# A new order for the attention period of a fused macaron block: two small operations change engine, one turn in the first feed-forward half comes a slot later

## The reference, cut to what matters

```
x = x + 0.5 * ffn(layernorm(x))          # shared SwiGLU + routed SwiGLU, 8 experts, top 1
x = x + attention(layernorm(x))          # (8, 512, 256), 16 heads of 16, 64 landmarks
x = x + 0.5 * ffn(layernorm(x))

# attention, for each of 8 batches
q_l, k_l = means of q, k over 8 neighbouring tokens          # landmarks
s1 = softmax(q @ k_l.T); s2 = softmax(q_l @ k_l.T); s3 = softmax(q_l @ k.T)
z = s2.T / (col * row)                                        # largest row and column sums
for _ in range(6):
    xz = s2 @ z
    z = 0.25 * z @ (13 I - xz @ (15 I - xz @ (7 I - xz)))
out = (s1 @ (z @ (s3 @ v))) @ Wo + bo
```

## Time and profile before

| | |
|---|---|
| median of 3 runs | 1190.49 us (1188.29 to 1193.56) |
| the profiled execution's own time | 1187.06 us |
| its span, first to last instruction | 1185.3 us |
| PE busy | 1096.0 us, 92% |
| DVE busy | 767.7 us, 65% |
| ACT busy | 581.3 us, 49% |
| POOL busy | 557.4 us, 47% |
| mean granted clock of PE | 0.970 of full speed |

### The profile page before, as it was taken

How to read it: one execution, slowest core, us unless ns; L and a number is a source line. 1 busy time by engine, 2 the same in 40 slices (tenths; PEclk the granted TensorE clock), 3 DMA queues, 4 the chain that set the end, 5 groups by cost and what they waited for, 6 DMA issues and landing times.

```text
span 1185.3 us, 30048 instructions
## 1 busy us (share of the span) xinstructions
PE 1096.0 (92%) x11278; PEld 886.9 (75%) x11279; DVE 767.7 (65%) x1425; ACT 581.3 (49%) x937; POOL 557.4 (47%) x774
## 2 busy tenths in 40 slices
PE   8999999999998778889889898879999999999997
PEld 6788887888887556667667676658888888888886
DVE  5746557767675755867877967545446566776764
ACT  4334246666664445355355453334434246666663
POOL 5710815666665623344434522224600717666664
PEclk8999999999999788999999998779999999999999
DMA  7181143222210400000000000012440142122220
GB/s 248 72 328 63 36 181 110 69 71 65 63 57 25 131 14 2 3 3 2 3 2 3 2 3 2 2 38 107 161 178 19 60 176 67 58 67 62 70 64 18
DMA packets 39472, 80.25 MB, mean 68 GB/s; under 512 B 6452, under 2 KB 31159, under 8 KB 38336
## 3 DMA queue, kind: packets, MB, share of 16 engines
q1 hardware_dynamic: 27568, 52.94, 12.4%
q0 software_dynamic: 11232, 25.20, 6.9%
q10 hardware_dynamic: 560, 0.52, 0.1%
HBM read 57.13 MB, written 27.00 MB: 71 GB/s over the span
## 4 chain that ended last, share of the span: by engine, by line
PE 78%; DVE 12%; ACT 3%; issue 3%; POOL 3%; DMA 1%; ACTq 0%; POOLq 0%; DVEq 0%; SPq 0%
PE PS L1730 18%; PE PS L1644 14%; PE PS L1744 12%; PE PS L1660 7%; PE PS L1737 3%; PE PS L1818 3%; DVE A_NM L805 3%; PE PS L1928 2%; PE PS L1575 2%; DVE A_NM L798 2%; PE PS L1678 2%; PE PS L1828 2%; PE PS L1941 2%; PE PS L1862 1%; PE PS L1671 1%
## 5 line engine op out<-in xcount | busy, mean ns | idle before, releaser
L1730 PE MATMUL PS<-WHL,XGH 128*128 128x512 f32 x624 | 217.6, 430 | 2.1 <-DVE WHL L676 2.1
L1485 POOL TENSOR_TENSOR A_W<-A_XC,CB 128x256 f32<-128x256 f32 x96 | 68.1, 730 | 207.3 <-DVE A_XC L891 181.3
L1744 PE MATMUL PS<-WD,XNT 128*128 x624 | 149.7, 383 | 1.5 <-ACT XNT L1135 1.5
L697 DVE SCALAR_TENSOR_TENSOR XNT<-PS,SCORES,XNT 128x512 f32<-128x512 f32 x78 | 58.6, 751 | 120.4 <-PE PS L1730 120.4
L1393 POOL DMA_INDIRECT X<-xs_dram,WHO x78 | 101.2, 1297 | 70.5 <-PE PS L1678 28.2
L1730 PEld LDWEIGHTS PS<-WHL,XGH 128*128 128x128 f32 x624 | 111.4, 189 | 20.2 <-DVE WHL L676 2.6
L1130 ACT ACTIVATE XNT<-PS,SCORES 128x512 f32<-128x512 f32 x78 | 53.7, 689 | 145.9 <-PE PS L1730 145.7
L1744 PEld LDWEIGHTS PS<-WD,XNT 128*128 128x128 f32 x624 | 112.6, 190 | 15.8 <-issue 2.0
L1730 PE MATMUL PS<-WHL,XGL 128*128 128x512 f32 x312 | 123.2, 395 | 0.0
L1387 POOL TENSOR_SCALAR XNT<-WD 128x128 f32<-128x128 f32 x64 | 49.2, 787 | 119.2 <-DVE WD L570 119.2
L1660 PE MATMUL PS<-SDH,HHL 128*128 128x256 f32 x512 | 103.7, 286 | 0.5 <-DVE X L610 0.5
(11 more groups left out here) (273 smaller groups left out, 2551.9 us busy)
## 6 DMA issues: line engine op xcount, KB each, us to landing
xs_dram<-WG SPq DMA_DIRECT2D x16, 512.0 KB, 3.0
WU<-in_r_up SPq DMA_DIRECT2D x2, 4096.0 KB, 14.8
shared_dram<-X SPq DMA_DIRECT2D x16, 512.0 KB, 3.3
WG<-in_r_gate SPq DMA_DIRECT2D x2, 4096.0 KB, 19.1
WD<-in_r_down SPq DMA_DIRECT2D x4, 2048.0 KB, 7.6
X<-in_x SPq DMA_DIRECT2D x7, 512.0 KB, 9.0
X<-mid_dram SPq DMA_DIRECT2D x7, 512.0 KB, 3.8
X<-xs_dram,WHO POOLq DMA_INDIRECT x78, 2.9
```

What stands on the lines that cost most here:

```text
L697: dve.scalar_tensor_tensor(B["RH"][:, u * F:(u + 1) * F], banks[3 + u][:], score(t), B["RS"][:, u * F:(u + 1) * F], ALU.mult, ALU.mult).th ...
L1485: pool.tensor_tensor(B["W"][:].rearrange("p (a m) -> p a m", m=M)[:, part, :], B["XC"][b % 2][:].rearrange("p (a w) -> p a w", w=XW)[:, pa ...
L1730: ins = pe.matmul(banks[bank][:], tok, w[:, k * F:(k + 1) * F], start=(k == 0 and i == 0), stop=(k == KD - 1 and i == 2))
L1744: ins = pe.matmul(banks[7][:, 0:D], B["HT"][:, u * F + f * P:u * F + (f + 1) * P], B["WD"][:, bass.ds(ex * (KF * D) + f * D, D)], start=(f ...
```

## The change

Nothing is computed differently. Five things change:

- PE's fillers stand in another order around the twelve products of a period, and so do DVE's and ACT's.
- `key_block` leaves DVE and becomes `key_landmarks` on ACT; `product_kept` (two copies of 128x64 out of PSUM) moves from DVE to ACT too.
- `column_max` is cut in three: the column maximum and its scaling stay, `pair_scale` (a reciprocal) comes between the two last reductions, and `masked_scale` (A_MR) moves into the next period, behind `chain_s(b, 3)`.
- The banks of turns and values are the same in all periods (turn k and value half jj in bank 6 + k, 6 + jj). Both halves of the values are projected behind the second round's second product; one half used to stand a round later.
- `TURN_SLOT` of groups 3 to 7 and everything behind them (logits, routing, table) comes one slot later, in both feed-forward halves. On POOL, `root(1, 0)` and `rows(1, 1)` of feed-forward 1 move behind other steps.

The core of the diff:

```diff
-    TURN_SLOT = {1: 2, 2: 4, 3: 5, 4: 7, 5: 8, 6: 9, 7: 10}
+    TURN_SLOT = {1: 2, 2: 4, 3: 6, 4: 8, 5: 9, 6: 10, 7: 11}
...
+            def key_landmarks(b):
+                act.wait_ge(att["lm"], count("lm", b, 4))
+                act.mul(B["KLS"][:], B["KL"][:], 1.0 / LM).then_inc(att["kls"], 1)
+
+            def product_kept(b):
+                act.wait_ge(att["tp_ready"], count("tp_ready", b, 1))
+                for c in range(KD):
+                    act.copy(B["XC"][b % 2][:].rearrange("p (a w) -> p a w", w=XW)[:, c * PC:(c + 1) * PC, M:],
+                             banks[c][:, 0:PC * HS].rearrange("p (a d) -> p a d", d=HS)).then_inc(att["tp"], 1)
...
                 chain_b(b, 2)
-                if exists(nxt) and nxt > 0:
-                    act.wait_ge(att["nm3_ready"], count("nm3_ready", nxt, 1))
-                    act.copy(B["NM3T"][:], banks[nm3_bank(nxt)][:, 0:P]).then_inc(att["nm3"], 1)
+                if exists(nxt):
+                    exp3(nxt, 0)
                 if exists(far):
                     projected(far, 0)
                     rounded(far, 0)
-                if exists(nxt):
-                    exp3(nxt, 0)
-                    if nxt > 0:
-                        values(nxt, 1)
...
                 chain_s(b, 4)
+                if exists(nxt):
+                    row_kept(nxt)
                 if exists(old):
                     heads_norm(old)
-                if exists(nxt):
-                    row_kept(nxt)
+                chain_x(b, 4)
+                if exists(nxt):
                     s1_max(nxt, 0, (0, 1))
-                chain_x(b, 4)
-                if exists(nxt):
-                    column_max(nxt)
-                    s1_max(nxt, 1, (0,))
                 chain_s(b, 5)
```

More of the change, by code:

```diff
@@ L855, in start_y @@
             def start_y(b):
+                dve.wait_ge(att["own"], count("own", b, 4))
                 dve.wait_ge(att["y0_ready"], count("y0_ready", b, 1))
@@ L891, in chain_x @@
                     dve.scalar_tensor_tensor(x, x, Y_KEPT, pairs(banks[c][:, 0:CW], XW)[:, :, low:], ALU.mult, ALU.add).then_inc(att["x"], 1)
-            def product_kept(b):
-                dve.wait_ge(att["tp_ready"], count("tp_ready", b, 1))
-                for c in range(KD):
-                    dve.tensor_copy(chain(b)[:, c * PC:(c + 1) * PC, M:XW],
-                                    banks[c][:, 0:PC * HS].rearrange("p (a d) -> p a d", d=HS)).then_inc(att["tp"], 1)
             def low_tokens(b, k):
@@ L994, in attention_vector @@
                 if exists(nxt):
+                    column_max(nxt)
+                    s1_max(nxt, 1, (0,))
+                    pair_scale(nxt)
                     s1_max(nxt, 1, (1,))
@@ L1004, in attention_vector @@
                 chain_x(b, 5)
+                if exists(nxt):
+                    start_y(nxt)
                 if exists(far):
@@ L1007, in attention_vector @@
                     query_block(far)
-                if exists(nxt):
-                    start_y(nxt)
-                    product_kept(nxt)
-                if exists(far):
                     landmarks(far, 1, 0)
@@ L1531, in attention_pool @@
                 chain_w(b, 4)
+                if b == NG - 3:
+                    root(1, 0)
                 chain_w(b, 5)
@@ L1991, in attention_tensor @@
                 chain_first(b, 0)
+                if exists(nxt):
+                    pe.wait_ge(att["bdr"], count("bdr", nxt, 1))
+                    pe.wait_ge(att["qkr"], count("qkr", nxt, 3))
+                    pe.wait_ge(att["y0"], count("y0", b, 2))
+                    s3_max(nxt, 0)
                 if exists(old):
@@ L2042, in attention_tensor @@
                 chain_second(b, 1)
-                if exists(nxt) and nxt > 2:
+                if exists(far) and nxt > 0:
+                    pe.wait_ge(att["xo"], count("xo", done, 1))
+                    turn(far, 1)
+                if exists(nxt) and nxt > 0:
                     pe.wait_ge(att["xtl"], count("xtl", nxt, 2))
-                    pe.wait_ge(att["xtl"], count("xtl", far, 2))
+                    pe.wait_ge(att["xtl"], count("xtl", far, 1))
                     pe.wait_ge(att["num"], count("num", old, 2))
@@ L2092, in attention_tensor @@
                     pv(nxt, 0)
-                    pe.wait_ge(att["e1"], count("e1", b, 2))
-                    s3_turned(nxt, 1)
+                chain_first(b, 3)
                 if exists(done):
@@ L2098, in attention_tensor @@
                     project(done, 1)
+                if exists(nxt):
+                    pe.wait_ge(att["e3"], count("e3", nxt, 2))
+                    pe.wait_ge(att["e1"], count("e1", b, 2))
+                    s3_turned(nxt, 1)
                 chain_second(b, 3)
+                if exists(far):
+                    pe.wait_ge(att["tts"], count("tts", nxt, 1))
+                    if far > 0:
+                        pe.wait_ge(att["qk"], count("qk", far, 1))
+                    project_qk(far, 1)
                 if exists(b):
@@ L2128, in attention_tensor @@
                 if exists(nxt):
+                    pe.wait_ge(att["rmax"], count("rmax", nxt, 2))
+                    spread_rows(nxt)
+                if exists(old):
+                    pe.wait_ge(att["rec"], count("rec", old, 1))
+                    pe.wait_ge(att["e1"], count("e1", b, 4))
+                    spread_denominators(old)
+                chain_second(b, 4)
+                if exists(nxt):
+                    pe.wait_ge(att["e3"], count("e3", nxt, 4))
+                    pe.wait_ge(att["rs"], count("rs", nxt, 1))
+                    pv(nxt, 1)
                     pe.wait_ge(att["ot"], count("ot", old, 2))
-                    pe.wait_ge(att["e3"], count("e3", nxt, 4))
+                    pe.wait_ge(att["e1"], count("e1", b, 4))
                     pe.wait_ge(att["qkr"], count("qkr", nxt, 2))
@@ L2141, in attention_tensor @@
                     column_sums(nxt)
-                    pe.wait_ge(att["s1m"], count("s1m", nxt, 2))
-                    s1_max(nxt, 1)
                 if b == NG - 1:
@@ L2151, in attention_tensor @@
                     first_turn(1)
+                if exists(nxt):
+                    pe.wait_ge(att["s1m"], count("s1m", nxt, 2))
+                    s1_max(nxt, 1)
                 if exists(far):
```

185 lines of the change are left out of this document (77 added, 108 removed).

## The result

The changed kernel takes **1156.26 us** (median of 4 runs, 1153.88 to 1157.66) against 1189.45 (1188.29 to 1193.56): ratio 0.971, 95% interval 0.968 to 0.974. Its profiled execution took 1155.66 us.

What follows compares the result with a forecast made beforehand. PE, busy 92% of the span, sets the time; only its waits and slow stretches can be won. 11.0 + 2.5 + 3 + 1.2 + 1.7 = 19.4 off 1190.49 gives 1171 us, range 1163 to 1184.

Steps and rivals of the forecast that it cites:

- The steady period: Period 4: PE's waits fall from 4.95 to 2.7 us, the period from 46.36 to 44.1, a gain of 2.2.
- the walk: Place-by-place check of period 4's filler against waits; new waits 0.4, 0.1 (exps), 0.8, 1.2 and 0.2 scattered.
- is not better than before: Round 6 to `start_y`: new waits of 0.8 and 1.2 us stand against the 1.09, 0.54 and 0.48 that go.
- periods 1 to 5 are close to this one: Each of periods 1 to 5 gains what period 4 does: 5 x 2.2 = 11.0 us.
- The moves worth nothing beyond 0.4 a period: A_KLS and the `product_kept` copies on ACT: worth 0 by themselves; without A_KLS's move some 0.4 us a period lost.
- Between 0 and 6 us; I take 3: Period 6: output projection fills the 2.23 us wait before round 2, whose low clock behind it cost 3 us; gain 3.
- the clock stays up: Rival, chance 0.07: clock stays up through periods 6 and 7, another 6 to 8 us, 1164 us.
- Periods -1 and 0: Period -1's 3.38 us wait for the exp of s3 gives about 1 back; 2.5 us for both, bounds 0 and 5.
- Feed-forward 0: Group 3's turn, a slot later, loses its 1.71 us wait for POOL's rows: gain 1.7, bounds 0 and 1.7.
- From period 7 on: Period 7: the projection moves into the 2.36 us wait before the first product: gain 1.2, bounds 0 and 1.6.
- The rival on the slower side: Chance 0.07: waits of 0.8 and 1.2 us at each period's end let the clock fall; 1203 us at 4.5 a period.
- signs of being wrong: An ACT exp wait of a us or more, low clock in periods 1 to 5, or a gather wait before the routed tiles.

Runs made afterwards that it cites:

- tail_whole: Changed kernel with the end of the period put back on PE and DVE as before the change, in every period: 1164.00 us.
- moves_back: Changed kernel with the scaling of the key landmarks and the copies of the kept product on DVE again: 1159.76 us.
- before_fill_6: Kernel before the change with 39 dummy transposes on PE in three waits of period 6: 1182.47 us, ratio to before 0.995.
- fill_end: Changed kernel with 35 dummy transposes on PE, before `start_y` in period 6 and around round 2's second product in period 7: 1150.97 us.
- proj_back_6: Changed kernel with the output projection's first half behind round 2's first product again, in period 6 alone: 1159.05 us.
- both_6: Changed kernel with, in period 6 alone, the output projection's first half and the period's end on PE and DVE as before: 1157.48 us.
- exp_behind: Changed kernel with ACT's first exp of s3 behind the far batch's first projection and its rounding again, in period -1 alone: 1159.07 us.
- best_2: Changed kernel with the old slot table and dummies in periods 6 and 7 and in the start's waits, none in periods -3 and -2: 1146.34 us.
- slots_old: Changed kernel with the old table of turns and routing steps in the feed-forward halves: 1155.34 us.
- fill_start_2: Changed kernel with dummies from feed-forward 0's end to period 0, by an error also in periods -3 and -2, 230 in all: 1163.95 us.
- tail_6: Changed kernel with the end of the period on PE and DVE as before the change, in period 6 alone: 1155.78 us.
- fill_start: Changed kernel with 18 dummy transposes on PE, 10 and 8 around the start of period 0: 1155.04 us.
- best: Changed kernel with the old slot table, dummies in periods 6 and 7 and at the start, by an error also in periods -3 and -2: 1157.53 us.

## Why the prediction was right, and where it failed

**What bounds the kernel** held: PE, its products unchanged, only waits and clock to be won.

**How far the sum was off.** The ledger has some 12 us more than the 19.4: 5.4 in period 6, 4.3 in periods 1 to 5, 2.9 in periods -1 and 0, 1.4 in the last stretch, and 1.8 less in the two feed-forward halves. Period 6 is the largest of these; no single term explains the miss alone.

**The steady period: right mechanism, size 0.6 us short.** Measured 2.8 in period 4 against 2.2, each wait at the place of the walk and the two on DVE smaller. Put back one by one, the output projection is worth 0.9 us, the end of the period 0.95 (period 5 of `tail_whole`), the two moves 0.44; the other 0.5 was not run alone. A wait of nearly that size stands in a row of period 4 before the change, which the walk had left among its "scattered" 0.6:

```profile
648.85 0.50 PE L1858 MATMUL PS<-A_NM3T,A_SEL 32*128 32x512 f32 x4 [0.42 <-ACT XNT L1222]
```

PE waited here for an exp, and after the change it does not; the walk had charged the exps 0.1 and had seen no such wait to be won. The sentence that this corner "is not better than before" was wrong: it charged DVE 4.4 us between the second `s1_max` and `start_y`, which were 4.0 (the column maximum with its scaling took 0.9 instead of 1.3, as DVE's rows above show), and the two waits came to 1.3 us, not 2.0, against the 2.1 that they replace. And "periods 1 to 5 are close to this one" held for 2 and 3 (2.8, 2.9), not for 1 and 5 (3.5, 3.3): 11.0 became 15.3. Period 1 before the change had two longer waits than period 4, 2.23 for POOL before the first product of round 3 and 1.43 for an exp, of which 1.26 is left; period 5 had 1.47 instead of 0.84 before that of round 2.

**The moves worth nothing beyond 0.4 a period**: measured 0.44. The rule of the Trainium skill that was weighed ("Perfetto Trace Analysis", Optimizing Scalar/DVE Operations) would have kept the scaling on DVE; that the median row and not its fast case held is what `moves_back` shows. The fast case is real (two of eight in the kernel before); what the working did not look for is what stands beside the long ones, POOL's A_W in every case.

**Period 6 is the step that failed.** "Between 0 and 6 us; I take 3" became 8.4, outside its own bounds. At full clock the old order takes 46.09 us (`before_fill_6`), the new 42.29 (`fill_end`): the order gives 3.8, close to the 3. The other 4.6 is clock: it cost 5.4 us before and 0.75 after. I had looked at one of three falls, the one in the earlier trace rows, and charged 3 us for it, where all three cost 5.4; the granted clock of 0.82 over 51 us says about 18 us of low clock, three times as much, and should have set the upper bound. With the projection in the wait the first fall is gone, and it is back, half as long, when the projection is taken out (`proj_back_6`). What removed the other two stays open: in one execution of `both_6` the waits before the first `s1_max` and the last second product stand beside falls again, but two of its four executions are as fast as the changed kernel. My rival "the clock stays up", at 0.07, came nearest, but only in part: low clock in periods 6 and 7 fell from 34.1 us to 13.7, not to none, and its 1164 was still too slow.

**Periods -1 and 0: 2.5 became 5.3.** I took about 1 off the 3.38 for the new order of the sums; `exp_behind` says that ACT's order alone is worth 3.4 at `start_t`. The wait itself is 2.7 of it (3.38 against 0.69). The rest comes right behind it, where the clock is low from 419.2 to 422.6: the products with the values take 1.93 us there instead of 1.10. Period 0 gave 2.1 although its clock was low for 13.7 us instead of 6.8; with the clock up, as in `best_2`, it would have been 5.0 (45.97 - 40.94).

**Feed-forward 0: 1.7 became 0.2.** "PE has little left there to give it back" was wrong. The 1.71 went, but the products behind the turn wait 0.89 for DVE and 0.48 for ACT, and at the first routed tile (180.43 before, 179.76 after) 0.7 is left of it, at the end 0.2. With the old table (`slots_old`) they start at 379.56 and 180.26 stands in place of 179.76: the slot itself is worth 0.5 us at the first routed tile and nothing at the end. A wait at the front of a stage that waits again later is not a gain.

**From period 7 on: 1.2 became 2.6**, outside its bound of 1.6, and by another mechanism. The first product of round 2 waits 0.73 us instead of 2.36, as forecast. But the projection that used to stand behind it is gone from there, and the second product now waits:

```profile
751.24 0.78 PE L1946 MATMUL PS<-A_BU,A_ST 64*64 64x80 f32 x32 [1.10 <-DVE A_ST L885]
```

In all PE idles for 7.85 us of this stretch (41.97 - 34.12) and idled for 7.94 before (44.53 - 36.59): the waits moved and gave 0.1. The other 2.5 is busy time, for fewer products run at low clock (a mean of 0.86 over 41.97 us is 11.8 us at half speed, against 16.9 before).

The rival on the slower side, falls of the clock behind the two waits at the end of each period, did not come: they are 0.64 and 0.68, and periods 1 to 5 have no low clock. `tail_whole` shows that it was a real one: with the old end, whose wait before the first `s1_max` is 1.47, falls came in four of them, and the median rose by 8 us. Of the signs of being wrong, one stands in the profile, a wait of 1.45 us on an exp, but in period 6 and of the size foreseen there.

## What to carry to other kernels

Read the granted clock of each stage before costing its waits: a mean of 0.82 over 51 us is 18 us at half speed, and the waits that brought it down are worth more than they last. Where a wait on the bounding engine can't be removed, work put into it, useful or dummy, can pay through the clock, but only if it ends before the wait would: the dummies gained some 8 us in `best_2` and lost 8 in `fill_start_2`, which also had them where nothing waited. An edit's gain at the front of a stage is to be followed to the stage's end before it is counted, and filler taken from behind a product can leave a new wait there. And one profile is one execution: where the clock falls differs between executions, so look at the granted clock and the time of each of them before a fall is put down to an edit.

## What was unexpected of the hardware

- PE's clock fell behind waits of 1.4 to 2.5 us, not only behind the 6.04 us for the first load. The Trainium skill ("TensorE: Matmul & The Clock Gate", HAM oscillation — how this bites in real kernels) tells of falls behind long waits for transfers; those here are waits of one engine for another. The length of a wait alone does not tell: behind the 1.39 and the 1.45 in period 6 of the changed kernel the clock stayed up, and in `both_6` it fell behind a wait of 1.49.
- The same order does not always fall in the same places. One stretch of 6.8 us cost period 4 of `before_fill_6` 2.7 us. The kernel before ran between 1183.4 us (mean granted clock 0.977) and 1195.1 (0.960) over these runs, the changed one between 1153.9 and 1157.7, and `best_2`, without any low clock from 383 us to feed-forward 1, between 1146.0 and 1146.8: much of the spread goes with the clock.
- The scaling A_KLS took 0.68 us in the median on DVE and 0.22 at best, in the kernel before and in `moves_back` alike, and 0.31 each time on ACT. All 13 long ones in these two traces ended 0.08 us after an A_W of POOL that had started just before them.
- The pause in period 3 stands at the same place of PE's instructions, not of the work: counted with the weight loads it is before the 12291st (in `tail_6` and `both_6` the 12290th), whether that belongs to the values or to `s1_max`, and it lasts 0.78 to 1.53 us. All 13 kernels with nothing put in ahead of it have it, the two old orders among them; the four that have dummies ahead of it (`fill_start`, `fill_start_2`, `best`, `best_2`) do not. What it is, no run shows.
